# SwiGLU stages: the down projection with its weights stationary and its result turned back

## What is computed

```python
gate = jnp.einsum('bsd,hd->bsh', x, wg)
up = jnp.einsum('bsd,hd->bsh', x, wu)
h = jax.nn.silu(gate) * up
return jnp.einsum('bsh,dh->bsd', h, wd)
...
x = x + 0.5 * _L1_ffn_ref(_layernorm(x, axis=-1), L1_ffn_w_gate, L1_ffn_w_up, L1_ffn_w_down)
```

## Time and profile before

| | us |
|---|---|
| median of three runs | 3133.98 |
| the three runs | 3133.33, 3133.98, 3147.24 |
| the profiled execution, its own time | 3120.58 |
| its span in the trace | 3118.8 |
| stage ffn1a, first gate/up to first matmul of the next stage | 880.9 to 980.6 |
| stage ffn1b, first silu to last scatter issued | 1843.9 to 2020.0 |

### The profile page before, as it was taken

One profiled execution on the slowest core, in us unless ns is written; L12 is line 12 of the kernel. 1 busy time (PEld: TensorE's weight loads), 2 busy tenths in 40 slices (PEclk: granted clock), 3 DMA queues, 4 the chain that ended last, 5 costly groups with the idle time before them and its releaser, 6 DMA issues. The chain is left out here.

```text
span 3118.8 us, 45117 instructions
## 1 busy us (share of the span) xinstructions
PE 2330.1 (75%) x13720; PEld 1446.9 (46%) x13720; DVE 2105.1 (67%) x5281; ACT 1459.4 (47%) x3113; POOL 920.3 (30%) x976
## 2 busy tenths in 40 slices
PE   2397689749767799899898977499575955577774
PEld 2397477648634122222222235389365954122223
DVE  3465788746544799999998824466674666587785
ACT  2265311126443388888887842166323653123222
POOL 4644235534413200000100004534274431131230
PEclk9999799869888699999999987699777977798987
DMA  4122100012211300000000000022211220000000
GB/s 143 43 66 67 40 8 15 18 34 63 79 34 34 128 19 20 19 19 18 19 19 17 7 29 25 30 61 62 59 40 44 64 86 0 23 0 0 0 0 28
DMA packets 112250, 115.54 MB, mean 37 GB/s; under 512 B 22064, under 2 KB 95504, under 8 KB 111248
## 3 DMA queue, kind: packets, MB, share of 16 engines
q1 hardware_dynamic: 93136, 71.44, 8.2%
q0 software_dynamic: 17408, 35.95, 3.4%
q10 hardware_dynamic: 1472, 5.27, 0.5%
HBM read 67.36 MB, written 44.83 MB: 36 GB/s over the span
## 5 line engine op out<-in xcount | busy, mean ns | idle before, releaser
L1732 DVE TENSOR_REDUCE attn_mx<-bank 128x1 f32<-128x512 f32 x1024 | 640.8, 682 | 61.0 <-PE bank L1511 52.8
L1633 ACT ACTIVATE attn_pT<-bank 128x512 f32<-128x512 f32 x1024 | 539.8, 604 | 126.7 <-PE bank L1526 126.3
L1511 PE MATMUL bank<-attn_K,attn_Q 48*128 48x512 bf16 x1024 | 336.4, 396 | 50.4 <-DVE attn_mx L1732 29.9
L1526 PE MATMUL bank<-attn_Q,attn_K 51*128 51x512 bf16 x1024 | 331.0, 386 | 2.5 <-ACT attn_pT L1633 1.4
L1539 PE MATMUL bank<-attn_pT,attn_vb 128*32 128x512 f32 x2048 | 276.2, 611 | 19.9 <-ACT attn_pT L1633 11.8
L1692 POOL TENSOR_TENSOR attn_m_rem<-attn_m_rem,attn_m_parts 8x128 f32<-8x128 f32 x128 | 53.3, 416 | 678.5 <-ACT attn_m_parts L1646 678.5
L1511 PEld LDWEIGHTS bank<-attn_K,attn_Q 48*128 48x128 bf16 x1024 | 71.8, 94 | 376.0 <-DVE attn_mx L1732 325.2
L2380 POOL TENSOR_TENSOR mix_rS<-mix_rT,mix_S 128x512 f32<-128x512 f32 x64 | 81.5, 1278 | 288.7 <-ACT mix_gT L2360 228.0
L903 PE MATMUL bank<-mix_prod_qk,ident 128*128 128x256 f32 x512 | 121.5, 392 | 0.0
L903 PEld LDWEIGHTS bank<-mix_prod_qk,ident 128*128 128x128 f32 x512 | 101.2, 199 | 25.2 <-issue 11.8
L2316 PE MATMUL bank<-mix_rS,mix_sel 128*128 128x512 f32 x128 | 73.8, 664 | 43.0 <-POOL mix_rS L2380 43.0
(11 more groups left out here) (610 smaller groups left out, 5927.3 us busy)
## 6 DMA issues: line engine op xcount, KB each, us to landing
ffn0a_x_ring<-xs_rows SPq DMA_DIRECT2D x72, 65.0 KB, 1.8
ffn0b_x_ring<-xs_rows SPq DMA_DIRECT2D x72, 65.0 KB, 1.8
ffn2a_x_ring<-xs_rows SPq DMA_DIRECT2D x72, 65.0 KB, 1.8
ffn2b_x_ring<-xs_rows SPq DMA_DIRECT2D x72, 65.0 KB, 1.8
w<-in_L_w ACTq DMA_DIRECT2D x2, 2048.0 KB, 16.3
ffn0a_y_back<-y_rows SPq DMA_DIRECT2D x8, 512.0 KB
ffn0b_y_back<-y_rows SPq DMA_DIRECT2D x8, 512.0 KB
w<-in_L_w SPq DMA_DIRECT2D x2, 2048.0 KB, 10.7
```

What stands on the lines that cost most here:

```text
L1511: nc.tensor.matmul(a_bank[n % 3][:], slot(net.Q, h, 0, KROWS)[:, qt * P:(qt + 1) * P], slot(net.K, h, 0, KROWS)[:, hf * CH:(hf + 1) * CH], ...
L1526: nc.tensor.matmul(s_bank[n % 3][:], slot(net.K, h, 0, KROWS + MROWS)[:, kt * P:(kt + 1) * P], slot(net.Q, h, 0, KROWS + MROWS)[:, hf * CH ...
L1633: nc.scalar.activation(pT[:, kt % RING, hf * CH:(hf + 1) * CH], s_bank[(n * HPB + hf) % 3][:], ACT.Exp, scale=HD ** -0.5).then_inc(exp_rea ...
L1732: nc.vector.tensor_reduce(mx[:, h % 2, qt, hf:hf + 1], a_bank[n % 3][:], AX.X, ALU.max).then_inc(a_used, 1)
```

## The change

In both SwiGLU stages the down projection now keeps the down weights stationary and moves the chunk's 512 tokens, so three matmuls take the place of twelve, and the result comes out with features across the partitions. ScalarE copies it from bank 4 into a new buffer `yT` (`turn_down`, after `norm.keep`), and a new step `flip` on TensorE transposes the four tiles back into bank 4. `flip(c)` stands between parts 0 and 1 of gate/up of chunk c + 1 (in the last chunk it follows the down projection, and in ffn1b the logits). `y_ready`, for which `add` waits, is now signalled by `flip`; `mult` waits for `yT_ready`, signalled by the down projection, before it writes `hs` again.

```diff
--- before.py
+++ after.py
@@ -1137,8 +1137,9 @@
         preloaded = part.sem("preloaded") if preload else None
         sg = part.sb("silu", [P, 2, CH])
         hs = part.sb("hs", [P, HC, CH])
-        gu_ready, silu_ready, h_ready, y_ready, y_added = (
-            part.sem(k) for k in ("gate_up_ready", "silu_ready", "h_ready", "y_ready", "y_added"))
+        yT = part.sb("yT", [P, CH])
+        gu_ready, silu_ready, h_ready, yT_ready, yT_kept, y_ready, y_added = (
+            part.sem(k) for k in ("gate_up_ready", "silu_ready", "h_ready", "yT_ready", "yT_kept", "y_ready", "y_added"))
         block = st.block()
 
         @block.sync
@@ -1163,10 +1164,16 @@
             def down(c):
                 pe.wait_ge(h_ready, (c + 1) * HC)
                 need(pe, y_added, c)
+                for j in range(HC):
+                    ins = nc.tensor.matmul(net.bank[4][:], net.L1_wd[:, j, :], hs[:, j, :], start=(j == 0),
+                                           stop=(j == HC - 1))
+                ins.then_inc(yT_ready, 1)
+
+            def flip(c):
+                pe.wait_ge(yT_kept, c + 1)
                 for i in range(TPC):
-                    for j in range(HC):
-                        ins = nc.tensor.matmul(net.bank[4][:, i * P:(i + 1) * P], hs[:, j, i * P:(i + 1) * P],
-                                               net.L1_wd[:, j, :], start=(j == 0), stop=(j == HC - 1))
+                    t = slice(i * P, (i + 1) * P)
+                    ins = nc.tensor.transpose(net.bank[4][:, t], yT[:, t], net.ident[:])
                 ins.then_inc(y_ready, 1)
 
             def body(c, depth):
@@ -1180,6 +1187,8 @@
                     norm.logits(pe, c - 1, router.rw)
                 if not is_last(c):
                     gate_up(c + 1, 0)
+                flip(c)
+                if not is_last(c):
                     gate_up(c + 1, 1)
 
             def tail(c):
@@ -1199,12 +1208,18 @@
                 act.wait_ge(gu_ready, c * HC + j + 1)
                 nc.scalar.activation(sg[:, j % 2, :], net.bank[(0, 1, 0)[j]][:], ACT.Silu).then_inc(silu_ready, 1)
 
+            def turn_down(c):
+                need(act, y_ready, c)
+                act.wait_ge(yT_ready, c + 1)
+                nc.scalar.activation(yT[:], net.bank[4][:], ACT.Copy).then_inc(yT_kept, 1)
+
             def body(c, depth):
                 silu(c, 0)
                 silu(c, 1)
                 silu(c, 2)
                 if depth > 0:
                     norm.keep(act, c - 1)
+                turn_down(c)
             deep_rounds(body, lambda c: norm.all_act(act, c))
 
         @block.gpsimd
@@ -1225,7 +1240,7 @@
         @block.vector
         def _(dve):
             def mult(c, j):
-                need(dve, y_ready, c)
+                need(dve, yT_ready, c)
                 dve.wait_ge(silu_ready, c * HC + j + 1)
                 nc.vector.tensor_tensor(hs[:, j, :], sg[:, j % 2, :], net.bank[(2, 3, 2)[j]][:],
                                         ALU.mult).then_inc(h_ready, 1)
```

## The result

| | before | after |
|---|---|---|
| median of four runs, us | 3137.12 | 3174.76 |
| lowest and highest, us | 3133.33 to 3147.24 | 3167.18 to 3178.85 |
| the profiled execution, its own time, us | 3120.58 | 3175.37 |
| its span, us | 3118.8 | 3173.6 |

The ratio is 1.0119, with a 95% interval of 1.0091 to 1.0146: the change costs 37.6 us, and it was forecast at 36 us. A fourth run of the kernel before has moved its median from 3133.98 to 3137.12 us. The two profiled executions lie further apart, 54.8 us, so the first thing to find out is how much of that belongs to the change. For this the rest of the text uses one measure, which stands for each stage in a window: from the first gate/up matmul to the last addition. Here are the two windows of the kernel before and then of the changed one.

What follows compares the result with a forecast made beforehand. The order of work around the down projection was taken to bind, with the addition as good as on the path. ffn1a 14.2 + ffn1b 15.4 + clock 6.6 = 36.2 us; 3134 + 36 = 3170 us, range 3152 to 3190.

Steps and rivals of the forecast that it cites:

- Down: Down projection in both stages: six wide instructions at 0.43 us each, saving 0.10 us a chunk, 1.6 us over 16 chunks.
- third rival: Wide columns are cheap: each down instruction takes the 0.111 us of a narrow one, time 3124 us; chance 0.02.
- Copy and transposes: After down: ScalarE's copy, 0.60 us, covered by gate/up part 0; four overlapping transposes take 0.49 us of TensorE.
- the rival in which they don't: Transposes don't overlap, or each shows as two instructions: 0.4 to 0.6 us in each of 15 chunks, 3178 us; chance 0.05.
- The late addition: Addition waits for the transposes behind gate/up part 0: 2.11 us later in ffn1a, 3.0 us in ffn1b's later crossings.
- the 4.8 us named among the signs: Sign of being right: in ffn1a the addition comes 4.8 us after the down starts, where it was 2.9.
- its 1.24 us: Last chunk of ffn1b: the addition's 1.24 us delay is covered, since the weights wait 3.15 us for GpSimd's exponent.
- where I had 6.6: ffn1b, gate/up part 2 to silu: longer pauses lower the clock in five later chunks, +6.6 us.
- in ffn1a ... I take nothing: Clock in ffn1a: a new pause of about 1.5 us before part 2 costs nothing, at most 1.7 us each of 7.
- less the 4.5 of slack: ffn1b, six later crossings: 18.0 us of delay less 4.5 us of ScalarE's idle time before the spreading, 13.5 us.
- The first rival: Half clock in ffn1a's part 2 (12 us) and ffn1b's part 2 through down (10 us): 3192 us; chance 0.13.
- The one that gives the clock back: Wide matmuls hold the clock: down takes 21.5 us and the 6.6 us falls away, 3142 us; chance 0.05.

Runs made afterwards that it cites:

- filled kernels: Matmuls whose result nobody reads put into TensorE's pauses: in the changed kernel 3136.09 us, ratio 1.0030; in the kernel before 3117.36 us, ratio 0.9979.
- the wide down alone: Kernel before with only the down projection made wide, no copy or transposes, result left unturned: 3132.56 us, ratio 0.9996.
- the bare late addition: Kernel before with one added wait, the addition also waiting for gate/up part 0 of the next chunk: 3177.61 us, ratio 1.0134.
- the early product: In ffn1b, next chunk's product 0 moved between statistics and choice of experts: kernel before 3117.95 us, ratio 0.9997; changed kernel 3143.85 us, ratio 1.0071.
- the transposes first: Changed kernel with the transposes right behind the down projection, ahead of logits and gate/up part 0: 3160.90 us, ratio 1.0082.

## Why the prediction was right

The time, 3174.76 us, is 4.8 us above the forecast, and 3.1 of these are the kernel before, whose median moved with its fourth run. The mechanism was right. The sum came out as well as it did because two of its terms missed in opposite directions, which is luck. Point by point:

**Down.** Right. 0.43 us an instruction, and a crossing at full clock 0.10 us shorter when it is changed alone, as computed. (In the third rival, the 62.5 us of down without the gain should be 62.8, 64.4 less 1.6; nothing hangs on it.) The Trainium skill's spacing of 131 ns at 512 columns ("TensorE: Matmul & The Clock Gate", Back-to-back issue gap) does not hold for these float32 instructions: the trace has 0.43 us.

**Copy and transposes.** Right. Copy covered by part 0, transposes 0.43 us. They overlap each other, so the rival in which they don't falls too.

**The late addition.** Right as a mechanism and, at full clock, as a size: 4.93 - 2.88 = 2.05 us (2.11 in the sum; the 4.8 us named among the signs was a slip: by the sum it should have read 4.99), and a crossing of 12.55 us where the forecast named about 12.7. In ffn1b, in a chunk whose down ran at full clock in both filled kernels, the addition starts 5.90 us after the down instead of 2.96, so 2.94 us later against 3.0. The end of ffn1b covered its 1.24 us: the last scatter follows the last addition by 33.2 us, before by 34.4. To that point ffn1b grew by 17.1 us.

**The clock, and ffn1b's order.** Here two sizes were off, in opposite directions. The filled kernels separate them, in ffn1a cleanly, since every down there ran at 1.00 in both. With the pauses filled, the changed kernel needs 101.65 + 147.96 = 249.6 us and the kernel before 88.38 + 139.95 = 228.3. So order and transposes are worth 21.3 us, 13.3 in ffn1a (forecast 14.2) and 8.0 in ffn1b (forecast 16.6 on this measure: 15.4 and the covered 1.2). The rest of the 35.5 us, 14.2, goes with the clock, where I had 6.6: the pauses cost the changed kernel 8.0 + 14.8 = 22.8 us and the kernel before 4.1 + 4.5 = 8.6.

The first failed step is "in ffn1a ... I take nothing" for the clock. Part 2, of which that sentence speaks, did run at 1.00 in all seven crossings, behind a pause of 1.19 us. What it left out is the down behind it: it ran partly at half clock in five crossings instead of three, 2 x 1.7 = 3.4 us by the crossings and 8.0 - 4.1 = 3.9 us by the windows.

The second is "less the 4.5 of slack" in ffn1b. In the five later crossings the forecast has 3.0 us each less 4.5, that is 10.5 us. With the pauses filled, those five take 97.6 us in the changed kernel (1890.72 to 1988.29) and 97.7 in the one before (1879.30 to 1976.98): no difference at all. The 8.0 us arise ahead of them, 3.1 until the first addition and 5.0 in the first two crossings. The slack at the spreading, which the earlier trace rows put at 4.5 us, was 7.9 us in the filled kernel before, and the change uses it up. The wait there, first in the filled kernel before, then in the filled changed one:

```profile
ACT ffn1b_norm_xn L242 <- DVE ffn1b_norm_shift L229: 7.9, 5, 3.2
...
ACT ffn1b_norm_xn L242 <- DVE ffn1b_norm_shift L229: 0.3, 2, 0.2
```

In both kernels VectorE still waits for GpSimd's exponent there (13.2 and 4.9 us), so the chain through GpSimd is the likely floor; that it is the floor was not tested. In ffn1b the split is rough. The fill was not the same in the two kernels and did not hold the clock at 1.00 (0.90 and 0.87): in the five later crossings all five downs of the filled kernel before ran wholly or partly at half clock, and two of the changed one. And 1.0 of the 8.0 us is a first down that came later after the first gate/up. How much of ffn1b's growth is order and how much clock stays open within some microseconds.

**The first rival**, the clock falling further, did not come true as written: in ffn1a part 2 stayed at 1.00, and it was the down that fell more often; in ffn1b part 2 and down of the later chunks ran at 0.50 to 0.63, not at half clock throughout. With 14.2 us the clock's share lies between my 6.6 and the 28.6 to which that rival comes (6.6 + 12 + 10). The one that gives the clock back is excluded by the wide down alone (PEclk 0.93 in ffn1a, as before).

Why ffn1b with the bare late addition takes 5.8 us more than the whole change stays open. The clock is lower there, 0.71 against 0.80. The pauses before part 2 are alike in the later crossings (4.80 and 4.87 us), so their length doesn't explain it.

## What to carry to other kernels

A new step is priced by who stands behind its reader: here three matmuls saved 0.10 us a chunk, and one hand-over moved behind 1.7 us of TensorE's own work cost ffn1a some 1.7 us a chunk at full clock, because VectorE does its list in order and had 0.26 us to spare. Before a stage is made later, look for the idle time of the next engine in line and subtract only that; and read it at the clock at which the stage will run, since here the same wait gave 4.5 us in one execution and 7.9 us with the pauses filled. And where TensorE pauses, ask what the pause does to the clock of the work behind it: idle time that costs nothing by the chain may cost there.

## What the runs showed of the hardware

Matmuls that nobody reads, put into pauses of 1.9 to 7.5 us, made two kernels' stages shorter: 22.8 us in the changed kernel, 8.6 us in the one before. In the changed kernel a crossing of ffn1a takes 14.25 us when its down runs partly at half clock, and 12.55 when it doesn't. The Trainium skill says in "TensorE: Matmul & The Clock Gate", Loop structure matters more than you think, that the loop nest decides whether matmuls stay warm; these runs agree as far as they go: with the same instructions in another order in the loop body, the granted clock of ffn1a was 0.87, 0.90 or 0.80.

The length of the pauses alone does not tell how often the clock falls. With the pause of 2.28 us before the turn alone, the kernel before had three slow crossings of seven in ffn1a, and two in the runs with the wide down alone and with the early product. With a second pause of 1.19 us before part 2 it was five, in the changed kernel and again in its run with the early product in ffn1b; with one of 1.26 us, under the bare late addition, it was six. With the transposes first the second pause was shorter, 0.75 us, and all seven were slow. Why that is so was not found out. The 7.3 us that this edit was computed to win back in ffn1a were lost to it: the stage came out 8.3 us above my number.
